# A macaron transformer on one core: the first attention joined with the gather and the sort of rows around it, the second gather moved inside the 32-expert layer, block weights split on chip

## The reference

```
x = x + 0.5 * ffn0(ln(x))      # 4 experts of 512, each token goes to one (argmax of a gate)
x = x + attn0(ln(x))           # linear attention: w = x @ qkv_w.T, one softmax over heads per token,
                               # out = -w * pi / (1 + dots), dots summed over a sequence; @ out_w + out_b
x = x + 0.5 * ffn0(ln(x))
x = x + 0.5 * ffn1(ln(x))      # 32 experts of 64, top 4 of sigmoid gates
x = x + attn1(ln(x))           # rope, softmax attention, 16 heads of 8
x = x + 0.5 * ffn1(ln(x))
```

## Time and profile before

| | |
|---|---|
| median of 3 runs | 2986.63 us |
| profiled execution, its own time | 2986.21 us |
| its span | 2984.2 us |
| PE, DVE, ACT, POOL busy | 78%, 65%, 46%, 32% |
| sort, blocks and gather of phase 0 | about 0 to 153, 153 to 324, 324 to 406 us |
| phase 1 | about 406 to 594 us |
| sort, blocks and gather of phase 2 | about 594 to 719, 719 to 889, 889 to 971 us |
| phases 3, 4, 5 | from 971 us to the end |

### The profile page before, as it was taken

The page is one execution under the profiler, slowest core; times in us unless marked ns, Lnnn a source line. Parts: engine busy times, 40 slices in busy tenths (PEclk is TensorE's granted clock), DMA queues, the critical chain, the costliest instruction groups (busy, mean ns, idle before and its releaser), DMA issues.

```text
span 2984.2 us, 39481 instructions
## 1 busy us (share of the span) xinstructions
PE 2339.5 (78%) x11474; PEld 1606.9 (54%) x11474; DVE 1950.5 (65%) x4504; ACT 1375.2 (46%) x2035; POOL 957.4 (32%) x894
## 2 busy tenths in 40 slices
PE   3378226654860799997899999999999999799999
PEld 3356114443650678785455555555555555477887
DVE  5344246653431688887677777777777777488887
ACT  0067113312760344443365665665666556344444
POOL 5600442273007455555111111111111110255554
PEclk9999657756995899998799999999999999799999
DMA  5555200013542688885000000000000000488887
GB/s 152 111 182 187 65 23 1 0 38 125 184 141 53 131 172 171 171 171 127 15 15 18 14 18 14 15 18 15 14 17 15 14 14 15 92 174 181 182 182 160
DMA packets 126476, 254.21 MB, mean 85 GB/s; under 512 B 19616, under 2 KB 24864, under 8 KB 120864
## 3 DMA queue, kind: packets, MB, share of 16 engines
q1 hardware_dynamic: 118176, 236.22, 33.0%
q0 software_dynamic: 8192, 16.79, 2.1%
HBM read 203.66 MB, written 32.52 MB: 79 GB/s over the span
## 4 chain that ended last, share of the span: by engine, by line
PE 47%; DVE 12%; DMA 11%; issue 10%; POOL 9%; ACT 6%; SPq 2%; POOLq 1%; DVEq 0%; ACTq 0%
PE ps L1777 10%; PE ps L1801 8%; DMA gate_rows<-gates_dram 7%; PE ps L1788 6%; PE ps L1510 4%; POOL sorted_x L630 4%; PE ps L1512 4%; POOL x_blk L639 4%; PE ps L1511 4%; DVE m L1255 3%; DMA w_blk<-w_dram 2%; DMA gates_dram<-gateT 2%; ACT g L756 1%; PE ps L1525 1%; PE ps L1850 1%
## 5 line engine op out<-in xcount | busy, mean ns | idle before, releaser
L1409 DVE TENSOR_REDUCE shift<-ps 128x1 fp32r<-128x512 f32 x1024 | 672.3, 686 | 142.3 <-PE ps L1777 135.3
L883 ACT ACTIVATE prob<-ps 128x1024 f32<-128x1024 f32 x512 | 524.8, 1026 | 379.0 <-PE ps L1788 374.8
L730 ACT ACTIVATE hi<-m 128x512 fp32r<-128x512 f32 x512 | 318.7, 631 | 408.9 <-DVE m L1255 408.8
L593 POOL TENSOR_TENSOR lo<-m,hi 128x512 fp32r<-128x512 f32 x256 | 348.5, 1365 | 369.5 <-ACT hi L730 369.5
L1777 PE MATMUL ps<-k_pad,q_st 128*128 128x512 f32 x1024 | 406.7, 439 | 29.6 <-DVE shift L1409 28.8
L1255 DVE SCALAR_TENSOR_TENSOR m<-ps,gate_rows 128x512 f32<-128x512 f32 x512 | 334.3, 681 | 99.6 <-DMA gate_rows<-gates_dram 50.7
L1777 PEld LDWEIGHTS ps<-k_pad,q_st 128*128 128x128 f32 x1024 | 179.8, 190 | 293.5 <-DVE shift L1409 263.8
L1788 PE MATMUL ps<-q_sh,k_pad 128*128 128x512 f32 x1024 | 332.1, 406 | 0.0
L1801 PE MATMUL ps<-prob,v_cols 128*32 128x512 f32 x2048 | 272.7, 605 | 0.4 <-ACT prob L883 0.4
L730 ACT ACTIVATE xnT<-ps 128x512 f32<-128x512 f32 x96 | 56.8, 591 | 466.5 <-PE ps L1517 258.4
L639 POOL DMA_INDIRECT x_blk<-sorted_y,y_row x128 | 120.9, 944 | 413.1 <-DMA sorted_y<-yb_rows 374.7
(11 more groups left out here) (204 smaller groups left out, 4079.0 us busy)
## 6 DMA issues: line engine op xcount, KB each, us to landing
gate_rows<-gates_dram SPq DMA_DIRECT2D x256, 512.0 KB, 12.1
w_blk<-w_dram SPq DMA_DIRECT2D x38, 1026.5 KB, 5.3
k_pad<-k_st SPq DMA_DIRECT2D x256, 64.0 KB, 2.0
x_blk<-sorted_x SPq DMA_DIRECT2D x38, 256.0 KB, 2.7
sorted_y<-yb_rows SPq DMA_DIRECT2D x38, 256.0 KB, 2.0
w_dram<-w_hl SPq DMA_DIRECT2D x16, 256.0 KB, 13.3
out<-x SPq DMA_DIRECT2D x16, 256.0 KB, 16.8
x<-in_x SPq DMA_DIRECT2D x1, 3584.0 KB, 14.8
```

Of the source, the lines that this page charges most:

```text
L593: pool.tensor_tensor(m["lo"][:, s], m["m32"][:, s], m["hi"][:, s].bitcast(F32), ALU.subtract).then_inc(sig(ph, "lo_pool"), 1)
L730: return act.activation(o, i, ACT.Copy)
L883: act.activation(prob[:, h % HP, 2 * half:2 * half + 2, :], ps[:, b0:b0 + 2, :], ACT.Exp, scale=SCALE).then_inc(sig(ph, "prob"), 1)
L1409: dve.tensor_reduce(shift[:, g % 2, b, c:c + 1], wide(PASS1 + b % 2), AXX, ALU.max, negate=True).then_inc(sig(ph, "qmax"), 1)
```

## The change

Three things are done. (a) The gather of phase 0, phase 1 and the sort of phase 2 become one loop that is written out: in one iteration t POOL scatters tile t-3 of phase 2, gathers tile t+6 of phase 0 and takes two roots, and DVE, TensorE and ACT do attention for tiles t to t+4 and the sort for tile t-2. The barrier between phases 0 and 1 stays in each engine's program behind the blocks; the gather now stands behind it. The bias sums of POOL go (a matmul with a row of ones does them), and so does the DVE sum with the gate's bias. The addition of the constant to the variance moves from POOL to DVE. (b) The gather of phase 2 goes into phase 3: three tiles ahead of its first tile, then one tile in its steps 6 to 9. (c) `w_dram` holds the weights once (128 x 1029 words per block) and is copied from DRAM to DRAM at the start; DVE splits each block's weights in the block loop (`split_w`) in two halves. Buffers of `x_blk` and `w_blk` are 3 instead of 4, `xnr` are 8 instead of 4. SP writes the zeros as soon as the totals are known and asks for weights ahead of rows.

The diff cut to its core: the sizes, SP's loads, POOL's joined loop, DVE's split and its block loop, POOL in phase 3, and DVE's joined loop, where `here(n)` says that tile t+n is one of the sixteen.

```diff
-XR = 4
-WB = 4
+XR = 8
+MOVES = 2
+WB = 3
...
-                def load(i):
-                    n, q = n0 + i, (n0 + i) % WB
-                    if i >= WB:
-                        sp.wait_ge(sig(ph, "yb_t"), n - WB + 1)
-                    e = sp.value_load(table[0:1, i:i + 1], min_val=0, max_val=E0 - 1)
-                    at = rows(i)
-                    sp.dma_start(x_blk[q][:], sorted_x[bass.ds(at, SEQ), :].rearrange("(p s) d -> p s d", s=BLK))\
-                      .then_inc(w_here[q], 16)
-                    sp.dma_start(w_blk[q][:].bitcast(F32), w_dram[bass.ds(e, 1)].rearrange("o p c -> p (o c)"))\
-                      .then_inc(w_here[q], 16)
+                def load_w(i):
+                    n, q = n0 + i, (n0 + i) % WB
+                    if i >= WB:
+                        sp.wait_ge(sig(ph, "yb_t"), n - WB + 1)
+                    e = sp.value_load(table[0:1, i:i + 1], min_val=0, max_val=E0 - 1)
+                    sp.dma_start(w_blk[q][:], w_dram[bass.ds(e, 1)].rearrange("o p c -> p (o c)"))\
+                      .then_inc(w_here[q], 16)
+                def load_x(i):
+                    q = (n0 + i) % WB
+                    at = rows(i)
+                    sp.dma_start(x_blk[q][:], sorted_x[bass.ds(at, SEQ), :].rearrange("(p s) d -> p s d", s=BLK))\
+                      .then_inc(x_here[q], 16)
...
                 for i in range(WB):
-                    load(i)
+                    load_w(i)
+                for b in range(MOVES):
+                    sp.wait_ge(moved[b], 512 * (turn + 1))
+                sp.wait_ge(filled, 16 * (2 * E0 - 1) * (turn + 1))
+                for i in range(WB):
+                    load_x(i)
                 for i in range(NB0):
                     save(i)
                     if i + WB < NB0:
-                        load(i + WB)
+                        load_w(i + WB)
+                        load_x(i + WB)
...
+            for t in range(-6, TILES + 3):
+                if here(-3):
+                    scatter(2, t - 3)
+                if here(-1):
+                    root(2, t - 1)
+                if here(6):
+                    collect(0, t + 6)
+                if here(4):
+                    root(1, t + 4)
...
+                def split_w(i, part):
+                    n = n0 + i
+                    c = slice(part * FF0, part * FF0 + FF0)
+                    if part == 0:
+                        dve.wait_ge(w_here[n % WB], 16 * (n // WB + 1))
+                    if part == 1 and n >= 2:
+                        dve.wait_ge(sig(ph, "yb"), n - 1)
+                    copy(w_hl[n % 2][:, 0, c], w_blk[n % WB][:, c]).then_inc(sig(ph, "w_split"), 1)
+                    dve.wait_ge(sig(ph, "w_split"), 4 * n + 2 * part + 1)
+                    sub(w_hl[n % 2][:, 1, c], w_blk[n % WB][:, c], w_hl[n % 2][:, 0, c].bitcast(F32))\
+                        .then_inc(sig(ph, "w_split"), 1)
...
                 for i in range(NB0):
                     for fb in range(FB0):
                         g_low(i, fb)
+                        if fb == 0 and i > 1:
+                            y_rows(i - 2)
+                        if fb == 1 and i + 1 < NB0:
+                            split_w(i + 1, 0)
                         if fb == 2 and i + 1 < NB0:
                             x_low_part(i + 1)
-                        if fb == 0 and i > 1:
-                            y_rows(i - 2)
+                        if fb == 3 and i + 1 < NB0:
+                            split_w(i + 1, 1)
...
+                    if ph == 3 and two_on and fb in (6, 7, 8, 9):
+                        collect_on(t, 1 - p, fb - 6)
...
+                for t in range(-5, TILES + 2):
+                    if here(1):
+                        scaled(t + 1)
+                    if here(2):
+                        apply_norm(1, t + 2)
+                    if here(-2):
+                        apply_norm(2, t - 2)
+                    if here(1):
+                        shifted(t + 1)
+                    if here(-1):
+                        add_y(t - 1)
+                        moments(2, t - 1)
+                    if here(1):
+                        softmax(t + 1, (t + 1) % 2)
+                    if here(2):
+                        x_low(ph, t + 2, t % 2)
+                    if here(-2):
+                        choose(2, t - 2)
+                    if here(0):
+                        minus_attn(t, t % 4)
+                    if here(5):
+                        add_back(0, t + 5)
+                    if here(4):
+                        moments(1, t + 4)
+                    if here(-2):
+                        place(2, t - 2)
+                    if here(0):
+                        attended(t, t % 4)
```

More of the change, by code:

```diff
@@ L658, in _ @@
+            pool.wait_ge(setup, 1)
+            for t in range(2):
+                root(0, t)
+            for t in range(TILES):
+                if t + 2 < TILES:
+                    root(0, t + 2)
+                scatter(0, t)
             barrier(pool, 1)
@@ L827, in attention0, with here @@
                 ph = 1
-                def step(t, k, here):
+                for t in range(-2, TILES + 2):
+                    def here(n):
+                        return 0 <= t + n < TILES
                     if here(0):
@@ new lines, in more, with logits @@
+            def more(dst, w, v):
+                return pe.matmul(dst, w, v, start=False, stop=True, skip_group_check=True)
+            def logits(ph, t):
+                lg = lg0(ph)
+                pe.wait_ge(sig(ph, "xnT"), FIRST[ph] + t + 1)
+                for b in range(BLK):
+                    pe.matmul(lg[:, b], ones_row[:], gate_b[:], start=True, stop=False)
+                    last = pe.matmul(lg[:, b], xnT0[:, b * P:b * P + P], gate_w[:], start=False, stop=True)
+                last.then_inc(sig(ph, "lg"), 1)
@@ new lines, in rank @@
+            def rank(ph, t):
+                hot = onehot[:, t * BLK:t * BLK + BLK]
+                pe.wait_ge(sig(ph, "hot"), FIRST[ph] + t + 1)
+                if t == 0:
+                    pe.matmul(ranks, rank_c[0:1, 2], rank_c[0:1, 3, 0:BLK * E0], start=True, stop=True)
+                last = more(ranks, rank_c[:, 0], hot)
+                for k in range(1, BLK):
+                    last = more(ranks[:, k:BLK], rank_c[:, 2], hot[:, 0:BLK - k])
+                last.then_inc(sig(ph, "rank"), 1)
@@ L1528, in ffn0, with count @@
+            def count(ph, t):
+                hot = onehot[:, t * BLK:t * BLK + BLK]
+                pe.wait_ge(sig(ph, "route_steps"), 5 * (FIRST[ph] + t + 1))
+                last = more(ranks, rank_c[:, 1], hot)
+                for k in range(1, BLK):
+                    last = more(ranks[:, 0:BLK - k], rank_c[:, 2], hot[:, k:BLK])
+                if t == TILES - 1:
+                    last.then_inc(sig(ph, "counted"), 1)
             def ffn0(ph):
-                base, turn = FIRST[ph], ph // 2
+                turn = ph // 2
@@ L1711, in attention0, with here @@
                 ph = 1
-                def step(t, k, here):
+                for t in range(-2, TILES + 3):
+                    def here(n):
+                        return 0 <= t + n < TILES
+                    if here(-3):
+                        count(2, t - 3)
                     if here(0):
```

555 lines of the change are left out of this document (272 added, 283 removed).

## The result

The kernel after the change takes 3157.28 us, the median of four runs (3155.83 to 3159.11), against 2988.57 for the kernel before on the same chip. The ratio is 1.056, with an interval of 1.054 to 1.058. The sign was forecast, the size was not: +169 us instead of +29, and 3157 lies above the range of 2955 to 3070.

The account below looks back on a forecast made before the run. Chains between engines, or one engine alone, bound the changed stages, the block loop being largest. Terms to phase 3's first root sum to 994.5 against 973.0, +21.5; with 8 in phase 3, +29.5, so 3015 us, range 2955 to 3070.

Parts of the forecast that it names:

- The block loop: Blocks of phases 0 and 2: rows land late behind the copy and save, period 15.3 us against 8.4.
- Rival 3: Blocks: the load is hidden anyway, period 8.7 us, 2804 us in all; chance 0.05.
- 14.5: Blocks: period in us before any clock cost, 2.97 to the copy, 6.0 to the transposes, 5.5 to the next `up`.
- the 0.8 for the clock: Blocks: us added per period for PE's low clock, a third of the 2.6 if all is low.
- The clock rival: Blocks: the clock stays low, 17.1 us per period, +58, 3073 us in all; chance 0.13.
- I take 15.5, nearer to the ceiling: Joined loop: us per tile, making its stage 294.8 us instead of 395.0, a gain of 100.
- The floor: Joined loop: at least 12.6 us per tile, from POOL's 8 indirect transfers and two roots.
- the ceiling: Joined loop: 16.6 us per tile if attention and sort do not overlap, 10.4 + 6.2.
- the second rival: Blocks at 14.1 us per period, joined loop at POOL's pace, 13.3 per tile, phase 3 free: 2943 us; chance 0.18.
- The 6.2 for the sort: Joined loop: us per tile for the sort of phase 2, used in the ceiling and where attention thins out.
- Price between 0 and 1.6 us for 14 tiles, 0 to 22: Phase 3: cost per tile of POOL's gathers in steps 6 to 9; 8 us taken in all.
- Rival 4: The joined loop does not overlap and phase 3 pays all: +27, 3042 us; chance 0.09.

Follow-up runs that it names:

- The filled kernel: Kernel after, with 24 matmuls of 512 columns, results overwritten, on PE ahead of each block's wait for rows from the fourth block on; 3105.63 us, ratio 1.038.

## Why the prediction was right in its sign and wrong in its size

**The block loop: right in mechanism, short in size.** The period was forecast at 15.3 and is 16.4. Loading ahead of the save took the loss away, and the kernel before shows the same loss with three buffers, so this cause is shown from both sides. Rival 3 (hidden anyway, 8.7) falls. The filled kernel splits the miss: "14.5" at the full clock is 14.86, all of the excess between copy and transposes (6.4 for 6.0), and the 0.8 for the clock is 1.6. Taking a third of the low level's price from phase 1's mean of 0.75 was the weak place. The 32 periods make 36 of the 36.7 us that the blocks were off.

**The clock rival: over half right.** It said the level stays low through the whole period, 17.1; it was 16.4. The Trainium skill, TensorE: Matmul & The Clock Gate, section HAM oscillation, has each turn of such a loop start at the low level. The trace agrees: all 16 blocks of each phase behind such a wait begin with transposes of 1.11 or 1.12 us. But PE is back at 0.39 per matmul 4.8 us later, so 1.6 of the 2.6 us was paid.

**The joined loop: the step that failed.** "I take 15.5, nearer to the ceiling" was 20.5. The floor came from POOL's work, the ceiling from the two old loops laid end to end, and in neither loop are biases added by matmuls. The change description names "a matmul with a row of ones" for each; the prediction gave it no price at all. Eight groups more per tile stand between the instructions of DVE that wait for PE and cost 6.6 us per tile (105 us over 16 tiles); with them the clock in the loop is 0.55, without them 0.64. The miss of this stage is 85.5 of the 142 us, and it is two errors that partly cancel: 105 us of biases that were put at nothing, less 20 us, because without them a tile takes 13.7 and not 15.5, near the 13.3 of the second rival. The ceiling of 16.6 excluded the truth, because it bounded the old work in a new order and not the new work. The loop without biases does lie between 12.6 and 16.6. The 6.2 for the sort in that ceiling has no row behind it either: with the 7.4 of its own row it would be 17.8, still below 20.5.

**Phase 3: the sign and place right, the bound too low.** "Price between 0 and 1.6 us for 14 tiles, 0 to 22" was 2.0 us per tile, and 27 us from the first root of phase 3 to the second of phase 4. It was said that in steps 6 to 9 POOL has more work than time; what was not said is that its root and norm in steps 10 to 12 come behind it, 2 us late in the tile shown. Leaving the transfers out gave back 24, moving them 19. Contention on the DMA engines, the other reason given, is not needed for these 19: the moved transfers share them as well. For the other 5 it was not tried. After this loss the unchanged phases 4 and 5 took 7.7 us less; see below.

**What held.** The gather of phase 2 (15.1, forecast 15.3), the stretches behind the blocks (22, forecast 21), the splits without a price, and in the start the last scatter, at 117.65 (forecast 117). The first transposes come at 133.4 and not at 127.4, and the 6 us lie behind that scatter: the weights are asked for at 125.45, when the zeros have been issued. Of the kernel after:

```profile
115.05 8.80 SPq L457 DMA_DIRECT2D sorted_x<-zeros  x7
125.45 2.60 SPq L473 DMA_DIRECT2D w_blk<-w_dram  x3
```

In traces of kernels that share this code the first transposes come between 129.3 and 134.6. In the two with 129.3 the zeros take 5.26 us to issue, in the others over 8. Why this differs is open.

**The other rivals.** Rival 4 (no overlap in the joined loop, phase 3 pays all) had the right places, and both its prices, 16.6 per tile and 22 us, were still too low. Of rival 2 only the pace per tile is borne out, and that without the biases alone.

## What to carry to other kernels

When a queue that is worked in order holds a wait and a prefetch behind it, that wait eats up part of the distance that the buffers give: four buffers were just enough here (0.21 us of waiting), three were not, and with the rows asked for a whole block earlier three were enough. Move the load ahead of the save before you take a buffer away. Price every instruction that a change adds by its count and shape, also where the text of the change presents it as a replacement; "the sum goes from POOL to a matmul" moved it from an engine with time to the one that the chain waits for. A stage's ceiling that is built from the old loops says nothing about instructions that neither of them has.

## What the runs showed of the hardware

- A wait of 5.9 to 6.7 us of PE per block was followed each time by matmuls at the low level (0.63 to 0.77 us for 512 columns against 0.39); waits of 1.8 us on average left the window's clock at 0.97, and with the wait filled it was 1.00.
- Float32 matmul groups at the low level take 0.51 us each (two of 128 columns) in a run of four, 0.72 when groups of one row and of 128 rows alternate. Groups with 4 columns take 0.24 in a run and 0.31 in alternation at the high level, and 0.47 and 0.52 at the low level.
- Phases 4 and 5 are the same code in both kernels, and from the second root of phase 4 to the end they take 1521.5 us before and 1513.8 after. The kernel before with three buffers has 1521.8, the ten variants of the kernel after 1512 to 1516 (one trace of each). The cause was not tried and is open.
